# Output weights of a state-space stage: high and low halves made by memory transfers instead of by ScalarE and VectorE

## What is computed

```python
x = x + xattn(layernorm(x), ctx, Wq, Wk, Wv, Wo)      # 32 heads over 2176 keys
x = x + mamba(layernorm(x), in_proj_w, conv_w, ..., out_proj_w)
x = x + ffn(layernorm(x), c1_w, c2_w, w1, w2t)        # one column of each block of 32 is kept
```

```python
proj = h @ in_proj_w.T                  # gate 8192, x 8192, B and C 2048, dt 128 columns
hBC  = silu(conv4(hBC)); dt = softplus(dt + dt_bias)
y = (decay-masked (C B^T)) @ (x * dt) + D * x         # per head, 128 heads of 64
y = y * rsqrt(mean(y * y) + eps) * norm_w
y = y * silu(gate)
return y @ out_proj_w.T                 # 8192 -> 512
```

## Time and profile before

| | us |
|---|---|
| median of 3 runs | 611.19 (611.17 to 611.98) |
| the profiled execution | 611.6 |
| its span | 609.9 |
| PE busy | 599.8 |
| DVE busy | 460.8 |
| ACT busy | 374.8 |
| POOL busy | 202.9 |

### The profile page before, as it was taken

How to read it: one execution, slowest core, us unless ns; L and a number is a source line. 1 busy time by engine, 2 the same in 40 slices (tenths; PEclk the granted TensorE clock), 3 DMA queues, 4 the chain that set the end, 5 groups by cost and what they waited for, 6 DMA issues and landing times.

```text
span 609.9 us, 10752 instructions
## 1 busy us (share of the span) xinstructions
PE 599.8 (98%) x3924; PEld 528.1 (87%) x3924; DVE 460.8 (76%) x911; ACT 374.8 (61%) x655; POOL 202.9 (33%) x164
## 2 busy tenths in 40 slices
PE   9999999999999999999999999999999999999997
PEld 8888888799998999899988889999989999997573
DVE  5613138678888888888886678879999998989783
ACT  5123125668677767776776735689688787787110
POOL 0000001259777877888785730220010000000000
PEclk9999999999999999999999999999999999999999
DMA  8501011878887888777876947647857768798400
GB/s 297 203 0 35 1 43 37 216 189 213 215 212 207 214 203 220 197 200 194 219 180 167 340 200 185 260 181 301 296 222 288 277 222 292 275 373 338 182 1 17
DMA packets 29968, 120.66 MB, mean 198 GB/s; under 512 B 7728, under 2 KB 8112, under 8 KB 22496
## 3 DMA queue, kind: packets, MB, share of 16 engines
q1 hardware_dynamic: 29488, 119.22, 62.2%
q10 hardware_dynamic: 432, 0.79, 0.4%
HBM read 86.30 MB, written 0.26 MB: 142 GB/s over the span
## 4 chain that ended last, share of the span: by engine, by line
PE 76%; DVE 9%; POOL 6%; ACT 4%; issue 3%; SPq 1%; DMA 0%; DVEq 0%; ACTq 0%
PE ps L1903 18%; PE ps L1594 11%; PE ps L1595 11%; PE ps L1596 11%; PE ps L1639 4%; PE ps L1701 4%; PE ps L1963 3%; POOL pt_lo L587 3%; PE ps L1777 2%; PE ps L1943 2%; PE ps L2075 2%; PE ps L1663 2%; POOL v_lo L587 2%; PE ps L2038 2%; DVE prob_far L1197 2%
## 5 line engine op out<-in xcount | busy, mean ns | idle before, releaser
L1903 PEld LDWEIGHTS ps<-norm_t,ring 128*128 128x128 f32 x1152 | 131.7, 192 | 2.9 <-issue 1.7
L1903 PE MATMUL ps<-norm_t,ring 128*128 128x128 f32 x1152 | 133.4, 276 | 0.0
L587 POOL TENSOR_TENSOR pt_lo<-far_t,pt_hi 128x512 fp32r<-128x512 f32 (+1 forms) x94 | 111.7, 1213 | 55.0 <-ACT pt_hi L690 54.9
L761 ACT ACTIVATE prob_far<-prob_far,neg_max 128x1024 f32<-128x1024 f32 (+2 forms) x96 | 85.5, 892 | 54.8 <-DVE neg_max L1201 54.8
L1197 DVE TENSOR_SCALAR_CACHE_REDUCE prob_far<-ps 128x256 f32<-128x256 f32 (+2 forms) x96 | 86.7, 906 | 32.1 <-PE ps L1596 31.6
L1221 DVE STREAM_TRANSPOSE prob_far<-prob_far 128x2176 f32<-128x2176 f32 x30 | 73.1, 2437 | 0.8 <-ACT prob_far L761 0.2
L1388 DVE SCALAR_TENSOR_TENSOR acc<-raw,cw,acc 128x127 f32<-128x127 f32 (+2 forms) x240 | 65.8, 351 | 3.7 <-ACT acc L944 3.1
L1594 PE MATMUL ps<-pt_hi,v_hi 128*128 128x256 f32 x208 | 61.3, 295 | 2.6 <-POOL pt_lo L587 2.3
L1594 PE MATMUL ps<-k_hi,q_hi 128*128 128x512 f32 (+2 forms) x160 | 61.4, 384 | 1.4 <-ACT v_all L690 0.7
L1596 PE MATMUL ps<-pt_lo,v_hi 128*128 128x256 f32 x208 | 58.9, 283 | 0.0
L1595 PE MATMUL ps<-pt_hi,v_lo 128*128 128x256 f32 x208 | 58.8, 283 | 0.0
(11 more groups left out here) (246 smaller groups left out, 1230.4 us busy)
## 6 DMA issues: line engine op xcount, KB each, us to landing
ring<-w_in_dram SPq DMA_DIRECT2D x36, 1024.0 KB, 5.1
far_t<-prob_far SPq DMA_DIRECT2D x240, 136.0 KB, 2.6
ring<-w_out_dram SPq DMA_DIRECT2D x16, 1024.0 KB, 5.0
ring<-wq_dram SPq DMA_DIRECT2D x16, 512.0 KB, 4.0
ring<-wo_dram SPq DMA_DIRECT2D x16, 512.0 KB, 3.6
w_sb<-w_dram SPq DMA_DIRECT2D x4, 896.0 KB, 10.5
ring<-w_dram SPq DMA_DIRECT2D x3, 1024.0 KB, 8.8
ring<-ctx_t_dram SPq DMA_DIRECT2D x2, 1024.0 KB, 5.4
```

The costliest lines, as they stand in the source:

```text
L587: sub = lambda dst, a, hi: pool.tensor_tensor(dst, a, hi, ALU.subtract)
L761: nc.scalar.activation(tile, tile, ACT.Exp, bias=neg_max[:, b, h:h + 1], accum_out=part_sum[:, b, h, i:i + 1]).then_inc(exp_ok, 1)
L1903: ins = mm(ps[:, bank, t * T:t * T + T], w[:, t, c, :], norm_t[:, c, :], start=(c == 0), stop=(c == NC - 1))
```

## The change

The output weights of the 11 split chunks no longer come through `SP` and are no longer subtracted by DVE:

- POOL issues a transfer from memory straight into `out_hi[i]`, whose type is float32r, so that it rounds (`high_load`). It waits until PE has freed the same chunk of the group before.
- ACT, where it copied, now writes the negative of `out_hi[i]` to `ring_lo[slot]` (`out_split`, scale -1). It waits for the transfer and for the slot.
- POOL, when ACT has counted `minus_ok`, issues a second transfer of the same 1 MB from memory that adds to `ring_lo[slot]` (`low_load`, `accum_op=ALU.add`).
- PE waits for that transfer (`out_low[i]`) where it waited for DVE.
- DVE's `out_split` is gone, and SP's loads of these chunks. SP's loop is written out.

```diff
--- before.py
+++ after.py
@@ -73,6 +73,8 @@
 DUOS = GROUPS // 2
 CELLS = 8
 OUT_SPLIT = (2, 2, 2, 2, 2, 1, 0, 0)
+LAST_SPLIT = 5
+SPLIT_LOADS = (6, 5)
 INTER = NH * 64
 
 FF = 1792
@@ -342,7 +344,8 @@
         w1_in, w1h_ok, w1l_ok, nh_ok, nl_ok = (sem("w1_in"), sem("w1h_ok"), sem("w1l_ok"), sem("nh_ok"),
                                                sem("nl_ok"))
         ug_ok, var_s = sem("ug_ok"), sem("var_s")
-        ugh_ok, ugl_ok, outh_ok, outl_ok = sem("ugh_ok"), sem("ugl_ok"), sem("outh_ok"), sem("outl_ok")
+        ugh_ok, ugl_ok, minus_ok = sem("ugh_ok"), sem("ugl_ok"), sem("minus_ok")
+        outh_in, out_low = [sem(f"outh_in{i}") for i in range(2)], [sem(f"out_low{i}") for i in range(2)]
         f_mask = sem("f_mask")
         stored = sem("stored")
 
@@ -553,15 +556,13 @@
 
             for j in range(4):
                 in_load(0, j)
-            with sp.Fori(0, 3) as turn:
-                for i in range(2):
-                    g = turn * 2 + (i + 1)
-                    in_load(g, 0)
-                    in_load(g, 1)
-                    out_load(turn * 2 + i, 0)
-                    out_load(turn * 2 + i, 1)
-                    in_load(g, 2)
-                    in_load(g, 3)
+            for g in range(1, GROUPS - 1):
+                in_load(g, 0)
+                in_load(g, 1)
+                for i in range(OUT_SPLIT[g - 1], 2):
+                    out_load(g - 1, i)
+                in_load(g, 2)
+                in_load(g, 3)
             for c in range(NC):
                 sp.dma_start(w1_sb[:, c, :], w1[c]).then_inc(w1_in, 16)
             for g in (GROUPS - 2, GROUPS - 1):
@@ -680,9 +681,45 @@
             pool.wait_ge(taps, 6)
             for k in range(4, 8):
                 left(k)
-            for q in range(1, DUOS):
-                pool.wait_ge(seg_ps, 4 * q - 1)
-                right(q)
+            w_out_rows = w_out.rearrange("n p f -> (n p) f")
+
+            def rows_of(g, i):
+
+                return w_out_rows[(2 * g + i) * P:(2 * g + i + 1) * P, :]
+
+            def high_load(g, i):
+
+                if g == 0 and i == 0:
+                    pool.wait_ge(gm_ps, 1)
+                if g:
+                    slot, before = out_chunk(g - 1, i)
+                    pool.wait_ge(freed[slot], before + 1)
+                pool.dma_start(out_hi[i][:], rows_of(g, i)).then_inc(outh_in[i], 16)
+
+            def low_load(g, i):
+
+                slot = out_chunk(g, i)[0]
+                pool.wait_ge(minus_ok, 2 * g + i + 1)
+                pool.dma_start(ring_lo[slot][:], rows_of(g, i), accum_op=ALU.add).then_inc(out_low[i], 16)
+
+            for g in range(LAST_SPLIT + 1):
+                if g == 0:
+                    high_load(0, 1)
+                if g % 2 == 0:
+                    pool.wait_ge(seg_ps, 2 * g + 3)
+                    right(g // 2 + 1)
+                if g == 0:
+                    high_load(0, 0)
+                if g == 1:
+                    low_load(0, 0)
+                    low_load(0, 1)
+                if g > 1:
+                    low_load(g - 1, 1)
+                if g:
+                    high_load(g, 0)
+                    if OUT_SPLIT[g] > 1:
+                        high_load(g, 1)
+                    low_load(g, 0)
 
 
         @block.scalar
@@ -971,8 +1008,10 @@
             def out_split(g, i):
 
                 slot, before = out_chunk(g, i)
-                act.wait_ge(landed[slot], (before + 1) * 16)
-                copy(out_hi[i][:], ring[slot][:]).then_inc(outh_ok, 1)
+                act.wait_ge(outh_in[i], (g + 1) * 16)
+                act.wait_ge(freed[slot], before)
+                nc.scalar.activation(ring_lo[slot][:], out_hi[i][:].bitcast(F32), ACT.Copy,
+                                     scale=-1.0).then_inc(minus_ok, 1)
 
             def ug_split(g, b, i):
 
@@ -1438,12 +1477,6 @@
                 dve.wait_ge(sq_ok, g + 1)
                 nc.vector.tensor_tensor(sq_sum[:], sq_sum[:], ysq[:], ALU.add).then_inc(sq_ok, 1)
 
-            def out_split(g, i):
-
-                dve.wait_ge(outh_ok, 2 * g + i + 1)
-                slot = out_chunk(g, i)[0]
-                sub(ring_lo[slot][:], ring[slot][:], out_hi[i][:].bitcast(F32)).then_inc(outl_ok, 1)
-
             def ug_split(g, b, halves):
 
                 n = 4 * halves
@@ -1479,11 +1512,7 @@
                     x_times_dt(g)
                 if g == 1:
                     ug_split(0, o, OUT_SPLIT[0])
-                if OUT_SPLIT[g - 1] > 0:
-                    out_split(g - 1, 0)
                 mask_decay(g + 1, o, 0)
-                if OUT_SPLIT[g - 1] > 1:
-                    out_split(g - 1, 1)
                 if g == GROUPS - 2:
                     dve.wait_ge(c2h_ok, 1)
                     sub(c2_st[64:64 + RANK, :], c2_sb[64:64 + RANK, :],
@@ -1948,16 +1977,16 @@
 
                 slot, before = out_chunk(g, i)
                 pe.wait_ge(ug_ok, 2 * g + i + 1)
-                pe.wait_ge(landed[slot], (before + 1) * 16)
                 if i < OUT_SPLIT[g]:
                     pe.wait_ge(ugl_ok, g + 1)
-                    pe.wait_ge(outl_ok, 2 * g + i + 1)
+                    pe.wait_ge(out_low[i], 16 * (g + 1))
                     high = out_hi[i][:].rearrange("p (t n) -> p t n", t=4)
                     low = ring_lo[slot][:].rearrange("p (t n) -> p t n", t=4)
                     for t in range(4):
                         ins = split_product(ps[:, 6, :], ug_hi[:, 4 * i + t, :], ug_lo[b][:, 4 * i + t, :],
                                             high[:, t, :], low[:, t, :], first and i == 0 and t == 0, False)
                 else:
+                    pe.wait_ge(landed[slot], (before + 1 - SPLIT_LOADS[i] * (g < GROUPS - 1)) * 16)
                     w = ring[slot][:].rearrange("p (t n) -> p t n", t=4)
                     for t in range(4):
                         ins = mm(ps[:, 6, :], ug[b][:, 4 * i + t, :], w[:, t, :], start=False,
@@ -2069,7 +2098,7 @@
                 if 0 < i < 3:
                     turn_over(i + 1)
                 s, before = stream(FFN0 + i)
-                pe.wait_ge(landed[s], 16 * (before + 1))
+                pe.wait_ge(landed[s], 16 * (before + 1 - (SPLIT_LOADS[i - 2] if i > 1 else 0)))
                 pe.wait_ge(ht_ok, i + 1)
                 for t in range(4 * i, min(4 * i + 4, NFT)):
                     ins = mm(ps[:, 4, :], hsel_t[:, t, :], ring[s][:, (t % 4) * DM:(t % 4 + 1) * DM],
```

## The result

| | us |
|---|---|
| before, median of 4 | 611.43 (611.17 to 611.98) |
| changed, median of 4 | 659.19 (658.45 to 663.78) |
| ratio | 1.0795, 95% interval 1.0777 to 1.0812 |
| forecast | 633, range 612.5 to 656 |

Slower, as forecast, but by 8.0% in place of 3.5% and outside the range. First the page of the changed kernel: busy time of the engines (against the earlier trace rows), POOL's queue, the chain that ended last, and the two kinds of transfer with their median time to landing.

What follows compares the result with a forecast made beforehand. PE, busy 98% of the span, was taken as the bound. From the profiled 611.6 us, + 7.5 (first step) + 13 (steps 2 to 5) + 1.5 (step 6) - 0.5 gave 633.1, forecast 633 us, range 612.5 to 656.

Steps and rivals of the forecast that it cites:

- What bounds the kernel, and the gain: State-space stage: PE is full, so removing 11 DVE subtractions gains at most PE's idle 0.48 us, taken as 0.5.
- The chain and its place: Steps 2 to 5: ACT's negation ends at t + 6.7, then issue and accumulation end at t + 14.8, 1.0 us late.
- The accumulation's own time: Adding transfer of 1 MB into ring_lo: 7.6 us for two operands per result, bounds 4.9 and 12.9.
- The step that failed: Steps 2 to 5: transfer supply of 27.0 us in a 23.76 us step, 3.2 us each, 13 us together.
- Theory A: Experiments' theory: an accumulation moves its bytes twice; what lies above that is other transfers in flight on the same engines.
- The first step: First step: accumulations land 5.0 and 7.5 us after PE wants them; PE loses 7.5 us, bounds 2.3 and 18.
- Step 6: Step 6: one accumulation beside the four feed-forward loads costs 1.5 us, bounds 0 and 4.
- The rounding load, at nothing: POOL's load into out_hi: lands in time for ACT, cost nothing; if late, up to 2 us a step.
- The plain cost: Rival: an accumulation costs what a load does, only the first step is late by 2.3 us, 613.4 us; chance 0.27.
- The slow accumulation: Rival: the accumulation takes 12.9 us or more, landing at t + 20.1 in steps 2 to 5, 663 us; chance 0.17.
- POOL held up at its issues: Rival: POOL's transfer issues are delayed, 2.1 us more in each of five steps, 643 us; chance 0.08.
- The sum by supply: Middle steps: 4 input chunks, 2 rounding loads and 2 accumulations of twice the time make 27.0 us of transfer.

Runs made afterwards that it cites:

- the kernel without adding: The changed kernel with the second transfer into ring_lo overwriting in place of adding, so the low half is wrong: 615.83 us, ratio 1.0092.
- The later order: The changed kernel with PE doing the output chunks of the split pairs behind the third input chunk, 3.6 us later in the step: 640.60 us, ratio 1.0475.
- the separate one: A kernel of transfers alone, computing nothing of the reference: an accumulation of 1 MB took 8.0 us alone, 10.3 beside one load, 13.6 beside three.
- The fill: The changed kernel with 18 matmuls of 128x128 on the identity ahead of the second output chunk of each split pair: 652.30 us, ratio 1.069.
- the version with one accumulation: The changed kernel with chunk 1's second transfer overwriting and only chunk 0's adding: 641.00 us; with PE's output chunks 3.6 us later, 625.09 us.

## Why the prediction was wrong

- *What bounds the kernel, and the gain.* Right: PE. With DVE's subtractions gone, steps 2 to 5 of the kernel without adding take 95.4 us in place of 95.8. The rounding load alone, which keeps the subtractions and takes ACT's copies away, gave 1 us. That is more than the 0.48 us of idle time that I had called the most there was to gain: step 2 alone became 0.7 us shorter, and the profile had shown 0.41 us of idle time there.
- *The chain and its place.* Right: ACT's negation ends at t + 6.8 (t + 6.7 forecast), the transfer follows, PE stands behind it in each step, most in the first. The later order moved the time as the chain says.
- *The accumulation's own time.* Right: 8.0 us alone, 7.6 taken. No row had it; the argument of two operands chose well between 4.9 and 12.9.
- *The step that failed: steps 2 to 5, "I take 3.2 for each of four steps, 13 us", with one load beside the second accumulation.* It was 33 us (8.2, 7.8, 9.6, 7.6). I had put one load beside it, at most 2.7 us, and otherwise relied on the mean supply of a step. But the mean says nothing of the moment. In the step at 450.48 these were issued between t and t + 20: the first accumulation at t + 0.4, the second at t + 7.2, three loads of SP at t + 0.2, t + 5.1 and t + 11.2, and the next rounding load at t + 16.2, so eight moves of 2.7 us if an accumulation counts twice. The engines were busy 1.00 of that time (0.95 to 1.00 in the three other steps). The first accumulation landed at t + 12.7 and the second at t + 20.0, not at t + 14.8 to t + 17.5; the three other steps are the same within a microsecond. Theory A is this, and holding SP's loads back, which brought the landing from 12.6 to 9.9 us and the time down by 20 us, is the test of it. The landings in company, 12.6 us in the kernel and 10.3 to 13.6 in the separate one, are that. About 6.1 us of each step's 8 are this lateness. Chunk 0, for which I had put nothing in these steps, was late as well, by 1.1 to 2.4 us.
- *What had no term: the clock.* Some 2.2 us a step. PE, which waits 4.2 to 4.5 us for a transfer, does its next twelve matmuls, or most of them, at the lower level. The prediction said the clock was full and didn't ask what a wait does to it. The fill shows the sign and, for a step, the size. A wait of 2 us did not always cost that: in the kernel without adding, the matmuls behind 2.08 us stayed 0.23 us apart; with SP's loads held back they slowed behind 1.94 us in step 3 and not behind 1.98 us in step 4.
- *The first step:* 11.3 us in place of 7.5. Chunk 0 was late by 5.5 (5.0 forecast), chunk 1 by 10.0 (7.5), and the clock was low after it. *Step 6:* 2.9 in place of 1.5.
- *The rounding load, at nothing.* Right by itself (5.0 us alone, the kernel with it alone is not slower, though its landing there is 9.8 to 10.1 us in the median). In the changed kernel it takes 7.6 and still is in time. With SP's loads held back it no longer was.
- *The rivals.* The plain cost is what the kernel without adding shows: 615.8 against 613.4. The slow accumulation, at 663, came nearest to the measured time, and its t + 20.1 is where the second accumulation landed, but by luck: it is not slow alone. POOL held up at its issues: not so.

Two errors of the same sign: crowding and the clock. The sum by supply, 27.0 us a step, held as a floor for the mean: three versions (held loads, later order, both) came down to 28.3 to 29.0 us in steps 2 to 5 and no lower. What stays open is why step 5 of the version with one accumulation is so long, and what the slower executions of the kernel without adding lost.

## What to carry to other kernels

A transfer that is issued late and wanted early is to be priced in its company: list all that is in flight at its issue or is issued before the moment it is wanted, and let it land when that has been moved. This is a price from above: beside three loads it would give 2.2 + 5 x 2.7 = 15.7 us, and the accumulation landed at 13.6. The mean load of the engines over a period gives a floor for the period, not a landing time. And if an engine that was always busy begins to wait some microseconds for something, look at what its clock does next: here a third again came on top of the lateness.

## What the runs showed of the hardware

An accumulating transfer from memory into SBUF takes 8.0 us for 1 MB and 5.5 for half, against 4.8 to 5.1 for a plain or rounding one; whether it rounds makes no difference (7.9 and 8.0). Its issue takes POOL 0.85 to 0.91 us, against 0.53 to 0.69 for a plain or rounding one. By the Trainium skill (Collectives: The Full Stack, The bandwidth ceiling) a reduction costs its second source read, 1.93 of a copy; by the slope, 5.0 us for 1 MB against the 2.3 of a load beside it, the trace agrees roughly. DVE copies of 128x2048 float32 ran at 1.2 us each beside an accumulation, which moved its landing from 8.0 to 8.2 us while its issue took 1.0 to 1.1 us in place of 0.87. The Trainium skill (SBUF — State Buffer, SBUF: two separate sides) has descriptors starved beside such copies, and a transfer that takes 620 ns alone takes 3100 ns in its example; these runs show 0.2 us on a transfer of 8.0.
